# Moving feed-forward steps between attention units and opening the last block's tail to seven PSUM banks

## The reference

```python
x = x + 0.5 * ffn(layernorm(x))
x = x + attention(layernorm(x))      # 16 heads of 16, causal, k and q layer-normed per head, softmax, Wo, bo
x = x + 0.5 * ffn(layernorm(x))      # the same weights as the first
```

## Time and profile before

| what | value |
|---|---|
| time, median of 3 runs (lowest, highest) | 1327.23 us (1325.44, 1329.65) |
| the profiled execution's own time | 1330.16 us |
| its span, first to last instruction | 1328.4 us |
| mean granted clock of PE | 0.946 of full speed |
| PE busy, share of the span | 1145.9 us, 86% |
| ACT busy | 1017.4 us, 77% |
| DVE busy | 468.8 us, 35% |
| POOL busy | 238.7 us, 18% |
| chain that ended last, by engine | PE 60%, ACT 16%, DVE 10% |

### The profile page before, as it was taken

The page is one execution under the profiler, slowest core; times in us unless marked ns, Lnnn a source line. Parts: engine busy times, 40 slices in busy tenths (PEclk is TensorE's granted clock), DMA queues, the critical chain, the costliest instruction groups (busy, mean ns, idle before and its releaser), DMA issues.

```text
span 1328.4 us, 22761 instructions
## 1 busy us (share of the span) xinstructions
PE 1145.9 (86%) x8884; PEld 367.9 (28%) x8884; DVE 468.8 (35%) x1180; ACT 1017.4 (77%) x1132; POOL 238.7 (18%) x377
## 2 busy tenths in 40 slices
PE   2646768899799969999799999899999999999984
PEld 2432322323232313322223223223222222212222
DVE  4655645456344423343233332322222212021113
ACT  3203546788688878898799899799999999999960
POOL 2223433323112210122101111101102101010000
PEclk9767888999899999999999999899999999999985
DMA  4011200201200030001200002100001200000000
GB/s 132 1 37 44 81 1 17 65 1 36 78 1 1 27 87 1 1 1 39 75 1 1 1 0 81 33 1 1 1 1 41 57 1 1 9 9 1 9 8 17
DMA packets 39672, 33.37 MB, mean 25 GB/s; under 512 B 8786, under 2 KB 39496, under 8 KB 39560
## 3 DMA queue, kind: packets, MB, share of 16 engines
q1 hardware_dynamic: 37360, 31.74, 8.2%
q10 hardware_dynamic: 2200, 0.12, 0.1%
HBM read 18.73 MB, written 12.85 MB: 24 GB/s over the span
## 4 chain that ended last, share of the span: by engine, by line
PE 60%; ACT 16%; DVE 10%; issue 7%; POOL 2%; DMA 1%; SPq 1%; ACTq 1%; DVEq 0%; POOLq 0%
PE ps L1127 56%; ACT ring L720 16%; PE ps L1169 2%; PE ps L1230 1%; DVE st L751 1%; DMA x<-in_x 1%; SPq L552 1%; DVE xnT L1115 1%; DVE xnT L792 1%; PE ps L1189 1%; POOL ring L674 1%; DVE area L1111 1%; DVE area L772 1%; POOL rstd L661 1%; DVE area L946 1%
## 5 line engine op out<-in xcount | busy, mean ns | idle before, releaser
L720 ACT ACTIVATE ring<-ps 128x1024 f32<-128x1024 f32 x1056 | 985.8, 1110 | 154.5 <-PE ps L1127 153.1
L1127 PE MATMUL ps<-ring,vf 128*17 128x512 f32 (+3 forms) x4608 | 564.8, 567 | 21.5 <-POOL ring L674 19.9
L1127 PE MATMUL ps<-queries,keys 50*128 50x512 f16 (+3 forms) x2304 | 380.2, 369 | 48.3 <-ACT ring L720 15.7
L1127 PEld LDWEIGHTS ps<-queries,keys 50*128 50x128 f16 x2304 | 94.0, 93 | 524.2 <-ACT ring L720 457.9
L674 POOL TENSOR_SCALAR_AFFINE_SELECT ring<-ring 128x256 f32<-128x256 f32 (+1 forms) x224 | 101.9, 473 | 453.9 <-ACT ring L720 451.8
L1127 PEld LDWEIGHTS ps<-ring,vf 128*17 128x17 f32 x4608 | 80.1, 96 | 190.2 <-issue 139.3
L1096 DVE STREAM_TRANSPOSE oT<-ps 128x512 f32<-128x512 f32 x32 | 22.9, 716 | 144.6 <-PE ps L1127 144.5
L661 POOL TENSOR_TENSOR rstd<-var,minus_half 128x4 f32<-128x4 f32 x24 | 24.4, 1019 | 266.9 <-DVE var L757 266.7
L1127 PE MATMUL ps<-baseT,xnT 128*128 128x256 f16 x384 | 59.6, 297 | 5.6 <-DVE qT L957 1.7
L924 DVE SCALAR_TENSOR_TENSOR x<-ps,power,x 128x512 f32<-128x512 f32 x32 | 24.0, 751 | 112.8 <-PE ps L1127 112.8
L790 DVE CAST xnT<-ps 128x512 f16<-128x512 f32 x34 | 23.5, 691 | 107.5 <-PE ps L1169 107.5
(11 more groups left out here) (150 smaller groups left out, 684.4 us busy)
## 6 DMA issues: line engine op xcount, KB each, us to landing
parts_d<-split SPq DMA_DIRECT2D x32, 256.0 KB, 2.6
keys<-parts_d SPq DMA_DIRECT2D x96, 64.0 KB, 2.4
queries<-parts_d SPq DMA_DIRECT2D x192, 32.0 KB
x<-in_x SPq DMA_DIRECT2D x8, 512.0 KB, 4.0
out_x<-x SPq DMA_DIRECT2D x16, 256.0 KB, 2.2
queries<-shift_d SPq DMA_DIRECT2D x64, 4.0 KB
ring<-in_base_W SPq DMA_DIRECT2D x1, 256.0 KB, 4.3
ring<-in_Wq SPq DMA_DIRECT2D x1, 256.0 KB, 6.5
```

What stands on the lines that cost most here:

```text
L720: act.activation(probs[:, u % RING, :], bank(2 * (u % SLOTS), 2), ACTF.Exp, bias=0.0, scale=1.0).then_inc(exp_ok, 1)
L1127: return pe.matmul(o, lhsT, rhs, start=start, stop=stop, skip_group_check=True)
```

## The change

Four edits. In the units of block c >= 3, `front(0, 0, c + 1)` and `prepare(c + 1)` begin at unit u0 + 6 instead of u0, with the same end. In the units of blocks 2 to 6, `back(c - 2)` and the load behind it end at u1 - 20 instead of u1 - 2; for block 7 nothing changes there. From the last exponential on, the stages that need a bank rotate over seven banks (all but ACC), each of which first waits for the last exponential. In block 7 the high parts of `turn2` and `turnin1` are copied by ACT, and the base matmuls of both `outer1` stages (24 of 36) are issued right behind `inner1`, ahead of `turnin1`; the rest of `outer1` adds to the same banks later.

```diff
--- before.py
+++ after.py
@@ -41,6 +41,7 @@
 XS = 4
 ACC, SIDE = 6, 7
 START_BANKS = (7, 5, 4, 3)
+END_BANKS = (7, 0, 1, 2, 3, 4, 5)
 NW = 7
 BLOCKS = (0, 2, 1, 3)
 FETCH = 8 * 16
@@ -184,14 +185,14 @@
         if c + 1 < NC:
 
             ahead = front(0, 0, c + 1) if c >= LONG else ()
-            lists.append(spread(itertools.chain(ahead, prepare(c + 1)), u0, max(u1 - 12, u0 + 6)))
+            lists.append(spread(itertools.chain(ahead, prepare(c + 1)), u0 + 6 if c >= LONG else u0, max(u1 - 12, u0 + 6)))
         if c + 2 <= LONG:
             lists.append(spread(front(0, 0, c + 2), u0, u1 - 2))
         if c >= 1:
             lists.append(spread(output(c - 1), u0 + 4, u0 + 8))
         behind = [c - 2] if 2 <= c < NC - 1 else [c - 2, c - 1] if c == NC - 1 else []
         if behind:
-            lists.append(spread(itertools.chain(*map(back, behind)), u0 + 10, u1 - 2))
+            lists.append(spread(itertools.chain(*map(back, behind)), u0 + 10, u1 - 2 if c == NC - 1 else u1 - 20))
         for u in range(UNIT0[c], UNIT0[c + 1]):
             side[u] = [q for steps in lists for q in steps.get(u, [])]
     values, groups, scored, split = [], [], set(), set()
@@ -272,6 +273,10 @@
         return n <= 3
     if stage in ("turn1", "value"):
         return n[0] <= 2
+    if stage == "turn2":
+        return n[0] == NC - 1
+    if stage == "turnin1":
+        return n == NC - 1
     return stage == "qk" and n // TC <= 2
 
 
@@ -295,7 +300,7 @@
 
 
 
-    def __init__(self, name, semaphore, order, banks, scalar, x, x_in, fronts):
+    def __init__(self, name, semaphore, order, banks, scalar, x, x_in, fronts, free=None):
         def s(q):
             return semaphore(f"{name}_{q}")
 
@@ -316,6 +321,10 @@
         held, count, rotate = {}, {self.read: 0, self.read_act: 0}, True
         for stage, n in order:
             rotate = rotate and stage != "scores"
+            if free and (stage, n) == ("exp", NU - 1):
+
+                rotate, banks = True, END_BANKS
+                held.update({b: free for b in END_BANKS if b != SIDE})
             if stage in BANK_STAGES:
                 i = len(self.use)
                 b = banks[i % len(banks)] if rotate else SIDE
@@ -453,7 +462,7 @@
         def x_main(c):
             return x_all[:, c % XS, :, :]
 
-        main = Pass("m", semaphore, ORDER, START_BANKS, on_scalar, x_main, lambda c: (x_in[c], 16), 2)
+        main = Pass("m", semaphore, ORDER, START_BANKS, on_scalar, x_main, lambda c: (x_in[c], 16), 2, (exp_ok, NU))
         gen = Pass("g", semaphore, [q for c in range(NC) for q in general_order(c)], (SIDE,), lambda *_: False, lambda c: xg,
                    lambda c: (gen_in, 16 * (c + 1)), 1)
 
@@ -1189,18 +1198,23 @@
                     m = pe.transpose(b[0:NR + 1, i * P:(i + 1) * P], h4[f][:, i, :], ident[:, :])
                 m.then_inc(K.ready, 1)
 
-            def outer(K, f, c, a):
+            def outer(K, f, c, a, parts=(0, 1)):
+
                 key = (f"outer{f}", (c, a))
-                b = side_bank(K, key)
+                b = side_bank(K, key) if 0 in parts else bank(K.bank[key])
                 pe.wait_ge(K.w_ok, 3)
-                pe.wait_ge(*K.done[f"turnin{f}", c])
+                if 1 in parts:
+                    pe.wait_ge(*K.done[f"turnin{f}", c])
                 for i in range(2):
                     t = slice((2 * a + i) * P, (2 * a + i + 1) * P)
                     o = b[:, i * D:(i + 1) * D]
                     for ib in range(2):
-                        mm_parts(o, lambda s: xnT[2 * f][:, s, ib, t], lambda s: baseT[:, s, ib, :], i == 0 and ib == 0, False)
-                    m = mm_parts(o, lambda s: hT[f][:, s, t], lambda s: bT[:, s, :], False, i == 1)
-                m.then_inc(K.ready, 1)
+                        if 0 in parts:
+                            mm_parts(o, lambda s: xnT[2 * f][:, s, ib, t], lambda s: baseT[:, s, ib, :], i == 0 and ib == 0, False)
+                    if 1 in parts:
+                        m = mm_parts(o, lambda s: hT[f][:, s, t], lambda s: bT[:, s, :], False, i == 1)
+                if 1 in parts:
+                    m.then_inc(K.ready, 1)
 
             def project(K, n):
                 c, t = n // TC, slice(n % TC * P, (n % TC + 1) * P)
@@ -1344,10 +1358,13 @@
                     turn(main, 2, *n)
                 elif stage == "inner1":
                     inner(main, 1, n)
+                    if n == NC - 1:
+                        for a in range(2):
+                            outer(main, 1, n, a, (0,))
                 elif stage == "turnin1":
                     turn_inner(main, 1, n)
                 elif stage == "outer1":
-                    outer(main, 1, *n)
+                    outer(main, 1, *n, (1,) if n[0] == NC - 1 else (0, 1))
 
 
 # ---- launch
```

## The result

| | before | after |
|---|---|---|
| median of four runs (lowest, highest), first set | 1328.38 us (1325.44, 1329.65) | 1290.01 us (1288.32, 1295.86) |
| profiled execution: own time, span | 1330.16, 1328.4 | 1288.32, 1286.5 |
| mean granted clock of PE | 0.946 | 0.966 |

The ratio is 0.9722 with a 95% interval of 0.9686 to 0.9758. A later set of six runs of the changed kernel, beside eleven of the one before, gave 1294.27 (1289.22 to 1295.64) against 1325.07 us, ratio 0.9748 (0.9715 to 0.9781). The forecast was 1289.6.

A forecast was written before the change was run, and what follows sets the result against it. PE and ACT were taken to hold the span, with DVE's late load of x stopping the exponentials. Starts 32.2, squeeze -4 and tail 9.4 sum to 37.6 us: 1327.23 - 37.6 = 1289.6, range 1281 to 1302.

The forecast's parts named there:

- Starts: First ten units of blocks 3 to 6: DVE's wait for x and what follows from it removed, 32.2 us gained.
- `moments0` hides under the `projout` matmuls: Block starts: its 1.41 us of statistics fit DVE's 1.72 us idle there, costed at nothing; uncovered, up to 1.4 us per block.
- Squeeze: Blocks 2 to 6 behind the tenth unit: back steps of blocks 0 to 4 in 18 units fewer, costing 4 us.
- Idle = a + b/n: ACT's idle time over n units behind the tenth, from blocks 3 and 6; b is 1260 us times units, pricing the squeeze.
- the bound of 10.6: Upper end of the squeeze's cost in us: all side work of blocks 2 to 6 pressed into 20 units fewer.
- Tail: From the last exponential on: steps sum to 8.6 us, with half of a possible clock gain 9.4, bounds 7 and 11.
- the clock's gain: Tail: at full clock the `turnin1` transposes and last twelve matmuls would save 0.5 and 1.2 us more; half was taken.
- A start like block 2's: Rival, chance 0.12: around u0 + 6 `moments0` delays the addition of `projout`, PE waits; price 12.4 us, time 1302.
- Base matmuls in the way of `turnin1`: Rival, chance 0.08: in the tail they overrun their gap by 1 to 2 us, tail gives 7 to 8; 1291.5.
- The load late: Rival, chance 0.03: SP reaches the moved load no earlier, behind a waiting `fetch`; only the tail gains, 1322 us.
- The side chain as the bound: Rival, chance 0.03: packed side stages sharing one bank cost blocks 2 and 3 84 us; 1370 us, slower.

The follow-up runs named there:

- kernel 2: The kernel before with only the six units' delay of front and prepare, back, load and tail as before; 1298.57 us, ratio 0.9772 to the kernel before.
- kernel 3: The kernel before with only the back and load ending at u1 - 20, front and prepare from u0, old tail; 1309.46 us, ratio 0.9865.
- kernel 5: The changed kernel with the seven banks in the tail, but high parts by DVE and base matmuls in their old place; one run, tail 38.8 us.
- 4: The kernel before with both the six units' delay and the back's earlier end, old tail; 1302.50 us, ratio 0.9819 to the kernel before.
- 6: The changed kernel with seven banks and early base matmuls, but the high parts copied by DVE; one run, tail 34.1 us.
- 9: The changed kernel with the back ending at u1 - 38 in place of u1 - 20; one run, 1293.54 us.
- 10: The changed kernel with the back of block 0 starting one unit later, at u0 + 11; one run, 1293.48 us.
- 1: The kernel before with the new tail alone, both lists at their old places; 1313.99 us, ratio 0.9891 to the kernel before.
- 7: The changed kernel with the back ending at u1 - 2 in all blocks; 1287.87 us, ratio 0.9696 to the kernel before.
- 8: The changed kernel with the back ending at u1 - 8 in blocks 3 to 6 and u1 - 2 in block 2; 1290.94 us, ratio 0.9726 to the kernel before.
- 11: The changed kernel with all back steps at their old places and the load alone moved to u1 - 9; 1281.73 us, ratio 0.9662 to the kernel before.

## Why the prediction was right

**Starts: right, by the mechanism given.** The chain through DVE, POOL and PE was read rightly, and the term was 33.0 for 32.2. The claim that `moments0` hides under the `projout` matmuls held: 12.1 to 12.3 us, as in block 7. What the prediction blurred is which edit does it. It put the earlier load first; kernel 2 shows that the six units' delay alone brings 30.2 of 33.0, and kernel 3 that the earlier back and load alone bring 25. The two overlap, since either one shortens or ends the stop. With `moments0` behind `turnout`, a load that is also in time is worth only 3 us more.

**Squeeze: wrong in mechanism and size.** The step that failed is "Idle = a + b/n", fitted to two blocks and scaled by the back's share to 4 us. The rows of before already spoke against it: by the fit (a is 2.6 us) block 2, with three quarters of the work over 74 units, should leave ACT idle for about 15 us, and the earlier trace rows have 10.65. Measured was 9.8, inside the bound of 10.6 that came from pressing all side work, but 6.8 of it lies in block 2, where I had 1.6 for the back. In its place the runs showed that the step's place decides: one collision at a head group's end was found and moved, for 2.7 of block 2's 6.9 us, and the rest stays open.

**Tail: right, a little small.** 10.9 for 9.4. `projout` gave 1.3 for 1.0 (2.32 us between its additions instead of 3.66), the second half at better clock. `turn2`: from the first transposes to the start of `inner1` 3.45 us (1268.01 to 1271.46) in place of 5.31 (1300.40 to 1305.71), 1.9 for 1.6. `turnin1` transposes took 0.66 for 1.17. `outer1`, from its first matmul behind `turnin1` to the last addition, took 2.3 us (1281.47 to 1283.74) where 3.5 were forecast and 9.5 were before, since its twelve matmuls took 1.47 us at full clock. That is 1.3 + 1.9 + 0.5 + 0.1 (ACT's copy) + 7.2 = 11.0. I took half of the clock's gain; all of it came. The page "TensorE: Matmul & The Clock Gate" of the Trainium skill (What's actually happening) says that activity releases the throttle; kernel 5's timeline agrees, with 1.49 and 0.87 us for the same six matmuls in one unbroken spell.

**The rivals.** A start like block 2's: not seen with the six units' delay; it is near what kernel 3 has (13.5 to 15.3). Base matmuls in the way of `turnin1`: not seen, 5.33 us as before. The load late: not seen. The side chain as the bound: not seen; even 36 units fewer cost 14.5 us in all, far from the 84 of that case.

**The sum.** 37.6 was forecast and 34.1 is what the windows give. The median of the first set differs by 38.4 us, that of the second by 30.8. That 1289.6 met 1290.01 so closely is luck: an underpriced squeeze (5.8 us) against underpriced starts and tail (0.8 and 1.5), and the runs' scatter for the rest.

## What to carry to other kernels

Where engines walk through one list in order, ask of a wait not how long it is but what stands behind it, on its own queue and on those that wait for that queue; moving the waiting step a few places back can be worth as much as making the data arrive earlier (here 30.2 us against 25, and the two overlap). Count the clock, too: here each such stop of PE was followed by work at half clock. Move the one instruction that is late (here a load with no arithmetic in it), and not the list that it ends: moving steps among a shared bank and a busy queue costs at places that no average over the block shows. A tail in single file gained more from more banks than the hand-overs alone would give, and PE came to full clock earlier in the work that had lost its pauses.

## What the runs showed that I had not expected

The first ten units of block 2, with the same plan in all kernels, took 13.70 us at a granted clock of 1.00 in some profiles (the changed kernel's first, 4, 5, 6, 9 and 10) and 15.2 to 15.3 at 0.89 in others (before, 1, 2, 3, 7, 8, 11 and the changed kernel's second), so the same instructions can fall on either side of a drop of PE's clock between two executions of one kernel. With the start of unit 72, between 244.1 and 250.8 us, this makes most of the scatter of single executions; what decides it stayed open.
